# Cross-attention by pairs of heads, with 64-row score products on the two halves of TensorE's array

## The reference

```python
x = x + xattn(layernorm(x), ctx, ctx, Wq, bq, Wk, bk, Wv, bv)   # the changed part
x = x + attn(layernorm(x), w_in, ...)                           # 16 heads of 32, position bias
x = x + ffn(layernorm(x), Wg, W1, W2, W3)                       # 8 experts, top 2

def xattn(Q, K, V, ...):           # H = 16 head slots, DK = 64; D = 512, so 8 heads
    q, k, v = proj(Q, Wq, bq), proj(K, Wk, bk), proj(V, Wv, bv)
    scores = einsum('bhqd,bhkd->bhqk', q, k) / sqrt(DK)
    out = einsum('bhqk,bhkd->bhqd', softmax(scores), v)
    return out.transpose(0, 2, 1, 3).reshape(B, -1, D_MODEL)
```

## Time and profile before

| | us |
|---|---|
| median of 3 runs | 1715.8 (1715.32 to 1717.26) |
| the profiled execution | 1716.57 |
| its span, first to last instruction | 1714.7 |
| TensorE busy | 1664.1 |
| VectorE busy | 1478.4 |
| ScalarE busy | 1282.5 |
| GpSimd busy | 407.4 |
| start, up to the loop's first scores | 50.3 |
| the loop's chunks with projections | up to 1345.5 |
| last chunk without projection | 1345.5 to some 1369 |

### The profile page before, as it was taken

The page is one execution under the profiler, slowest core; times in us unless marked ns, Lnnn a source line. Parts: engine busy times, 40 slices in busy tenths (PEclk is TensorE's granted clock), DMA queues, the critical chain, the costliest instruction groups (busy, mean ns, idle before and its releaser), DMA issues.

```text
span 1714.7 us, 39194 instructions
## 1 busy us (share of the span) xinstructions
PE 1664.1 (97%) x13412; PEld 1000.6 (58%) x13412; DVE 1478.4 (86%) x2349; ACT 1282.5 (75%) x3167; POOL 407.4 (24%) x500
## 2 busy tenths in 40 slices
PE   6999999999999999999999999999999687999998
PEld 3555555555555555555555555555555465777776
DVE  6999999999999999999999999999999846776765
ACT  4788888888888888888888888888888634655554
POOL 3233233232232232332232332332332100000000
PEclk9999999999999999999999999999999875999999
DMA  6455555555555555554555555555564670465551
GB/s 240 78 127 125 108 122 104 124 115 116 128 105 122 107 123 125 106 125 100 128 122 108 124 104 122 114 119 125 108 124 81 112 240 1 149 219 186 211 192 50
DMA packets 442396, 215.93 MB, mean 126 GB/s; under 512 B 416736, under 2 KB 422880, under 8 KB 435568
## 3 DMA queue, kind: packets, MB, share of 16 engines
q1 hardware_dynamic: 442064, 215.07, 51.9%
q10 hardware_dynamic: 288, 0.27, 0.1%
HBM read 111.96 MB, written 0.56 MB: 66 GB/s over the span
## 4 chain that ended last, share of the span: by engine, by line
PE 95%; DVE 2%; ACT 1%; DMA 1%; issue 1%; POOL 0%; SPq 0%; DVEq 0%; ACTq 0%; POOLq 0%
PE ps_proj L864 59%; PE ps_s L829 10%; PE ps_proj L946 9%; PE ps_o L845 8%; PE ps_o L969 4%; PE ps_s L902 1%; PE ps_proj L882 1%; PE ps_proj L913 1%; DVE wsp L661 1%; DMA ctx_f<-ctxt_dram 1%; PE ps_o L889 0%; PE ps_o L813 0%; POOL ctx_s L305 0%; PE ps_proj L923 0%; PE ps_s L793 0%
## 5 line engine op out<-in xcount | busy, mean ns | idle before, releaser
L864 PE MATMUL ps_proj<-ctx_s,wk_s 128*128 128x512 f16 x2352 | 541.5, 380 | 9.1 <-POOL ctx_s L305 9.0
L864 PE MATMUL ps_proj<-wv_s,ctx_s 128*128 128x512 f16 x2352 | 539.3, 379 | 0.0
L305 POOL TENSOR_TENSOR ctx_s<-ctx_f,ctx_s 128x512 f16<-128x512 f32 x196 | 272.8, 1393 | 894.7 <-ACT ctx_s L355 894.7
L394 ACT ACTIVATE prob<-ps_s,nmax 128x256 f32<-128x256 f32 x784 | 364.9, 470 | 113.0 <-DVE nmax L587 101.9
L864 PEld LDWEIGHTS ps_proj<-ctx_s,wk_s 128*128 128x128 f16 x2352 | 217.6, 98 | 244.0 <-POOL ctx_s L305 9.4
L864 PEld LDWEIGHTS ps_proj<-wv_s,ctx_s 128*128 128x128 f16 x2352 | 217.0, 98 | 232.3
L580 DVE TENSOR_REDUCE cmax<-ps_s 128x2 f32<-128x512 f32 x392 | 269.4, 687 | 62.5 <-PE ps_s L829 55.6
L597 DVE SCALAR_TENSOR_TENSOR k_s<-ps_proj,bk_s,k_s 64x512 f16<-64x512 f32 x392 | 294.0, 750 | 12.2 <-ACT k_s L363 3.1
L606 DVE SCALAR_TENSOR_TENSOR p_s<-prob,p_s 128x512 f16<-128x512 f32 x392 | 268.7, 685 | 7.7 <-ACT p_s L387 1.6
L387 ACT ACTIVATE p_s<-prob 128x512 f16<-128x512 f32 x392 | 247.0, 630 | 4.9
L829 PE MATMUL ps_s<-k_s,q_s 128*128 128x256 f16 x1568 | 236.9, 274 | 4.4 <-ACT prob L394 4.2
(11 more groups left out here) (119 smaller groups left out, 1154.6 us busy)
## 6 DMA issues: line engine op xcount, KB each, us to landing
ctx_f<-ctxt_dram SPq DMA_DIRECT2D x49, 1024.0 KB, 5.3
wst<-w_dram SPq DMA_DIRECT2D x96, 512.0 KB, 4.2
pt_s<-p_s SPq DMA_TRANSPOSE x392, 3.1
w_in_sb<-w_in_dram SPq DMA_DIRECT2D x1, 3072.0 KB, 11.8
tisa<-tisa_scores SPq DMA_DIRECT2D x3, 1024.0 KB, 14.5
w_f<-wk_dram SPq DMA_DIRECT2D x1, 1024.0 KB, 7.5
w_f<-wv_dram SPq DMA_DIRECT2D x1, 1024.0 KB, 11.6
w_f<-wq_dram SPq DMA_DIRECT2D x1, 1024.0 KB, 13.4
```

The costliest lines, as they stand in the source:

```text
L305: pool.tensor_tensor(out=ctx_s[odd][1][:, t, :], in0=ctx_f[odd][:, t, :], in1=ctx_s[odd][0][:, t, :], op=ALU.subtract).then_inc(ctx_low, 1)
L394: ins = act.activation(prob[:, u % 4, r * HC:(r + 1) * HC], ps_s[:, u % 2, r * HC:(r + 1) * HC], ACT.Exp, bias=nmax[odd][:, col:col + 1], ...
L864: ins = pe.matmul(ps_proj[:, u % 4, :], lhsT, rhs, start=(t == 0 and n == 0), stop=(t == DT - 1 and n == 2))
```

## The change

The loop goes by pairs of heads g = 0 to 3 (NG = 4) instead of heads.

- **K** stays as the projection leaves it: ScalarE writes the whole 128-row block's high part in one instruction, VectorE the low part in one, to a tensor of their own (k_s[i][0], k_s[i][1]). q is no longer doubled.
- **Scores** of a pair: for each row class, three products of 64 rows for each of the two heads, the heads in turn, head 0 in rows 0 to 63 into bank 0 of ps_s, head 1 in rows 64 to 127 into bank 1. That is 12 products of 64 rows for 8 of 128. A pair uses both banks, so the next pair's scores wait for all its exponentials.
- **Softmax**: one max and one nmax of four columns, four exponentials in a row, one P high and one P low of 1024 columns. prob and p_s have two buffers for four. P high and P low of a pair stand in the pair's own step, behind its exponentials (before: in the next step).
- **Transposes**: two DMA transposes per pair, the high and the low part of both heads, the high one behind P high already. PV_LAG is 2 pairs.
- **Projections**: two blocks per step, 2g behind the scores and 2g+1 behind P·V; their high and low parts are placed to match.

```diff
-PV_LAG = 5
+NG = NB // 2
+PV_LAG = 2
 # SyncE
-                sp.wait_ge(p_low, NB * c + u + 1)
-                sp.sem_inc(may_turn, 1)
-                sp.dma_start_transpose(pt_s[:, u, :, :, :].rearrange("p k b q -> p (k b) q"),
-                                       p_s[:, u % 4, :, :].rearrange("p k c -> p (k c)")).then_inc(turned_p[u], 16)
+                for k, split in enumerate((p_high, p_low)):
+                    sp.wait_ge(split, NG * c + g + 1)
+                    sp.sem_inc(may_turn, 1)
+                    sp.dma_start_transpose(pt_s[:, g, k, :, :], p_s[:, g % 2, k, :]).then_inc(turned_p[g], 16)
 # ScalarE, K high
-                    act.activation(k_s[odd][0:64, 2 * g, :], ps[0:64, :], ACT.Identity, bias=bk_s[0:64, g:g + 1])
-                    act.activation(k_s[odd][64:128, 2 * g + 1, :], ps[64:128, :], ACT.Identity,
-                                   bias=bk_s[64:128, g:g + 1]).then_inc(proj_high, 1)
+                    act.activation(k_s[odd][0][:, g, :], ps, ACT.Identity, bias=bk_s[:, g:g + 1]).then_inc(proj_high, 1)
 # ScalarE, the new step
+                for g in range(NG):
+                    pc, pg = (c, NB - 1) if g == 0 else (c + 1, 2 * g - 1)
+                    if exists(pc, 0):
+                        proj_highs(pc, pg, odd if g == 0 else 1 - odd)
+                    if exists(c, 2):
+                        ctx_highs(c + 2, odd, (g,))
+                    if exists(c, -1) and g == 0:
+                        alphas(c - 1, 1)
+                    if exists(c, 0):
+                        act.wait_ge(nmax_done, NG * c + g + 1)
...
+                        for b in range(2):
+                            for r in range(2):
+                                col = 4 * g + 2 * b + r
+                                ins = act.activation(prob[:, g % 2, (2 * b + r) * HC:(2 * b + r + 1) * HC],
+                                                     ps_s[:, b, r * HC:(r + 1) * HC], ACT.Exp, bias=nmax[odd][:, col:col + 1],
+                                                     scale=LOGIT_SCALE, accum_out=lsum[odd][:, col:col + 1])
+                        ins.then_inc(exp_done, 1)
+                    if exists(c, 1):
+                        proj_highs(c + 1, 2 * g, 1 - odd)
+                    if exists(c, 0):
+                        act.wait_ge(exp_done, NG * c + g + 1)
...
+                        act.activation(p_s[:, g % 2, 0, :], prob[:, g % 2, :], ACT.Copy, scale=P_SCALE).then_inc(p_high, 1)
+                        if g == 1:
+                            alphas(c, 0)
 # VectorE, the new step: max, nmax, then
+                    pc, pg = (c, NB - 1) if g == 0 else (c + 1, 2 * g - 1)
                     if exists(pc, 0):
+                        proj_lows(pc, pg, odd if g == 0 else 1 - odd)
                     for half, (dc, dodd) in ((1, (c - 1, 1 - odd)), (0, (c, odd))):
+                        if g == (0 if half else 1) and exists(dc, 0):
...
                             dve.tensor_tensor(dmax[:, cols], nmax[dodd][:, cols], nmax[1 - dodd][:, cols],
                                               ALU.subtract).then_inc(dmax_done, 1)
+                    if exists(c, 1):
+                        proj_lows(c + 1, 2 * g, 1 - odd)
+                    if exists(c, 0):
+                        dve.wait_ge(p_high, NG * c + g + 1)
+                        dve.scalar_tensor_tensor(out=p_s[:, g % 2, 1, :], in0=prob[:, g % 2, :], scalar=P_SCALE,
+                                                 in1=p_s[:, g % 2, 0, :], op0=ALU.mult, op1=ALU.subtract).then_inc(p_low, 1)
+                    if g in (0, 2) and exists(c, -1):
+                        half, n = g // 2, 2 * (c - 1) + g // 2
...
                         dve.tensor_tensor(acc, acc, ps_o[:, half, :], ALU.add).then_inc(added, 1)
 # TensorE, scores
-                        for r in range(2):
-                            for part in range(2):
-                                ins = pe.matmul(ps_s[:, u % 2, r * HC:(r + 1) * HC], q_s[part][:, u, r * P:(r + 1) * P],
-                                                k_s[odd][:, u, r * HC:(r + 1) * HC], start=(part == 0), stop=(part == 1))
+                        if g >= 1 or after(c, -1):
+                            pe.wait_ge(exp_done, NG * c + g)
+                        for r in range(2):
+                            for n, (a, b) in enumerate(THREE):
+                                for head in range(2):
+                                    rows = slice(DK * head, DK * head + DK)
+                                    ins = pe.matmul(ps_s[:, head, r * HC:(r + 1) * HC], q_s[a][rows, g, r * P:(r + 1) * P],
+                                                    k_s[odd][b][rows, g, r * HC:(r + 1) * HC], start=(n == 0), stop=(n == 2))
+                        ins.then_inc(s_done, 1)
+                    project(c, odd, 2 * g)
...
+                    project(c, odd, 2 * g + 1)
```

More of the change, by code:

```diff
@@ L61, in after, with back @@
     return not isinstance(c, int) or c + n >= least
-def back(c, u, lag, per=NB):
+def back(c, u, lag, per=NG):
     return (c, u - lag) if u >= lag else (c - 1, u - lag + per)
@@ new lines, in split_q, with proj_lows @@
+                ins = dve.tensor_tensor(q_s[1][:, :, :], q_f[:, :, :], q_s[0][:, :, :], ALU.subtract)
+                ins.then_inc(q_ready, 1)
+            def proj_lows(c, g, odd):
+                dve.wait_ge(proj_high, NB * c + g + 1)
+                ps = ps_proj[:, g % 4, :]
+                if g < 4:
+                    dve.scalar_tensor_tensor(out=k_s[odd][1][:, g, :], in0=ps, scalar=bk_s[:, g:g + 1], in1=k_s[odd][0][:, g, :],
+                                             op0=ALU.add, op1=ALU.subtract).then_inc(proj_low, 1)
+                else:
+                    dve.tensor_tensor(v_s[odd][1][:, g - 4, :], ps, v_s[odd][0][:, g - 4, :],
+                                      ALU.subtract).then_inc(proj_low, 1)
@@ L575, in step @@
             def step(c, odd):
[L576 removed]
+                for g in range(NG):
                     if exists(c, 0):
[L579 to L580 removed]
+                        dve.wait_ge(s_done, NG * c + g + 1)
+                        dve.tensor_reduce(cmax[:, g % 2, :], ps_s[:, :, :].rearrange("p b (r k) -> p (b r) k", r=2), AX,
@@ L603, in step @@
-                    tc, tu = back(c, u, 1)
-                    if exists(tc, 0):
-                        dve.wait_ge(p_high, NB * tc + tu + 1)
-                        dve.scalar_tensor_tensor(out=p_s[:, tu % 4, 1, :], in0=prob[:, tu % 4, :], scalar=P_SCALE,
-                                                 in1=p_s[:, tu % 4, 0, :], op0=ALU.mult, op1=ALU.subtract).then_inc(p_low, 1)
+                        proj_lows(pc, pg, odd if g == 0 else 1 - odd)
                     for half, (dc, dodd) in ((1, (c - 1, 1 - odd)), (0, (c, odd))):
-                        if u == (0 if half else 4) and exists(dc, 0):
+                        if g == (0 if half else 1) and exists(dc, 0):
@@ L815, in project_q, with project @@
                 ins.then_inc(q_done, 1)
+            def project(c, odd, u):
+                if not exists(c, 1):
+                    return
+                if u == 0:
+                    pe.wait_ge(ctx_low, DT * (c + 2))
+                if isinstance(c, int) and c == -1 and u in (0, 4):
+                    pe.wait_ge(w_split, 1 + u // 4)
+                if u >= 4 or after(c, 0):
+                    pe.wait_ge(proj_low, NB * c + NB + u - 3)
+                cs = ctx_s[1 - odd]
+                for t in range(DT):
+                    for n, (a, b) in enumerate(THREE):
+                        if u < 4:
+                            lhsT, rhs = wk_s[a][:, t, u * P:(u + 1) * P], cs[b][:, t, :]
+                        else:
+                            lhsT, rhs = cs[b][:, t, (u - 4) * P:(u - 3) * P], wv_s[a][:, t, :]
+                        ins = pe.matmul(ps_proj[:, u % 4, :], lhsT, rhs, start=(t == 0 and n == 0),
+                                        stop=(t == DT - 1 and n == 2))
+                ins.then_inc(proj_done, 1)
@@ L867, in step @@
-                    if isinstance(c, int) and c == -1 and u == 1:
+                        if vg % 2 == 0 and after(vc, -1):
+                            pe.wait_ge(added, 2 * vc + vg // 2 - 1)
+                        for head in range(2):
+                            u = 2 * vg + head
+                            for r in range(2):
+                                col = (u % 4) * 2 * DK + r * DK
+                                for i in range(2):
+                                    tile = 2 * r + i
+                                    for n, (a, b) in enumerate(THREE):
+                                        ins = pe.matmul(ps_o[:, vg // 2, col:col + DK], pt_s[:, vg, a, 4 * head + tile, :],
+                                                        v_s[vodd][b][:, tile, u * DK:(u + 1) * DK],
+                                                        start=(i == 0 and n == 0), stop=(i == 1 and n == 2))
```

162 lines of the change are left out of this document (44 added, 118 removed).

## The result

| | before | after |
|---|---|---|
| median of 6 runs each on one chip, us | 1715.8 (1715.32 to 1717.26) | 1723.42 (1722.25 to 1724.74) |
| profiled execution, its span | 1716.57, 1714.7 | 1723.75, 1722.0 |
| TensorE, VectorE, ScalarE busy | 1664.1, 1478.4, 1282.5 | 1661.5, 1090.8, 1095.7 |
| first scores of the loop | 50.34 | 50.55 |
| first scores of the last chunk | 1345.52 | 1344.51 |

A forecast was written before the change was run, and what follows sets the result against it. TensorE was taken to bound the kernel before and after, with the other engines just hidden. +2 us over the loop and +9 at the end gave +11 on the median of 1715.8: 1727 us, range 1706 to 1800.

The forecast's parts named there:

- The switches: TensorE's score bursts: each change between full and 64-row products costs 0.10 us, 0.20 per burst, eating the gain.
- Rival 2: Score bursts on TensorE: shape changes cost near zero, so the kernel gets faster, 1706 us; chance 0.14.
- The offset of the second half: Score burst on TensorE: 0.02 us added for the array's second half, within a burst of 0.88 against 0.875.
- The halves overlap: Scores on TensorE: 12 products of 64 rows take 6 slots, 0.656 us for 0.875, saving 0.219 per pair.
- The ring: Loop cycle max, nmax, exponentials, K/V high, P high, P low, next max: 26.3 to 26.7 us per chunk, under TensorE's 27.0.
- Meetings of nmax with GpSimd: VectorE's nmax held up by GpSimd multiplications in the loop: 0.3 to 0.6 us per chunk of a possible 1.65.
- rival 1: In the loop, the ring of ScalarE and VectorE replaces TensorE as the bound: 28.5 us per chunk, 1798 us; chance 0.27.
- A late pair without cost: Loop: a pair may be late once free; 5.9 us of other TensorE work against 3.4 leaves 2.2 us of cover.
- The transposes: DMA transposes, two per pair: about five us of cover before P·V needs P low, so no cost.
- The last chunk: No projection hides the ring there: 26.4 us from first scores to the last P low's end, against 18.0, so +8.4.
- the 0.7 by which the ring was to be late: Last chunk: 0.7 us of ring lateness counted in the 26.4 us to the end of the last P low.
- The last P·V: End of the last chunk: 24 products instead of 12 at the half clock, some 0.06 us each, +0.7.

The follow-up runs named there:

- the first experiment: Changed kernel with score products ordered three of head 0, then three of head 1 per row class, instead of heads in turn: 1725.21 us.

## Why the prediction came out as it did

Predicted 1727.0, faster/same/slower at 0.12/0.13/0.75; measured 1723.4, slower. The sum was +2 in the loop and +9 at the end; measured −1.2 and +8.2, with +0.3 at the start and behind.

- **The switches, 0.10 a side.** Right, and the step on which the sign hung: 0.10 in and 0.10 out in the trace, 0.107 and 0.105 from the runs that added and removed one. Rival 2 falls.
- **The offset of the second half, 0.02.** Too much: both halves start within a hundredth. That is the loop's miss: a burst of 0.87 instead of 0.88, and so per pair a hair less than the 0.875 removed instead of 0.01 more; the loop came out a little shorter where it was to be a little longer. Over 192 pairs a hundredth is 2 us, most of the 3.2 between +2 and −1.2. The term was priced right in kind and set a hundredth or two too high.
- **The halves overlap.** Right, and more robust than I had thought: the first experiment, which should have taken it away, didn't.
- **The ring, 26.3 to 26.7 clean.** At its lower edge: 26.4 as read in one chunk with its brush, 26.2 to 26.3 clean by the three runs with an extra max. Inside it K high costs 0.57, since P high starts that long after it, and not 0.70; the other steps are within 0.03.
- **Meetings of nmax with GpSimd, 0.3 to 0.6 per chunk.** Fewer: 4 x (194 − 160) ns = 0.14 in the mean. The walk through the chunk had the right places: 0.24 instead of 0.16 at the first pair, a near miss at the third; it missed a small one at the fourth (0.23 in some chunks). But its argument that the meeting thins out when the ring lags was wrong, and this was an argument against rival 1. A slowdown of rival 1's kind, the ring in TensorE's place, was 0.08 us away: an extra 0.14 per pair brought it on, at +35 us. The prediction had left the third pair open ("possibly"), and no step of it worked out whether they meet there; that they don't was luck.
- **A late pair without cost.** The prediction has 2.2 us of cover after one late pair; its own terms, 5.9 less 3.4, give 2.5. Nothing here tests it alone, and no sum uses it.
- **The transposes, nothing.** TensorE waits for none in the loop (it is busy throughout). Right.
- **The last chunk, 26.4 to the end of P low, +8.4.** Measured 25.5 (1344.51 to 1370.01), +7.5. The steps were right: 5.62 predicted, 5.64 measured. Two terms of the sum were too high: the 0.7 by which the ring was to be late (its max starts right behind the first burst), and 0.2 of the first scores.
- **The last P·V, +0.7.** Right: 1.48 for 24 products, 0.83 for 12 before, +0.65.

So the fall in VectorE's and ScalarE's work had no effect because neither bound the kernel; TensorE's saving of 0.22 per pair was eaten by two changes of shape; and folding two steps into one, with nothing left to hide it in the last chunk, made the difference of the medians.

## What to carry to other kernels

When products are cut to a part of the array so that two run side by side, add 0.2 us for each burst before counting the gain, and make bursts long: at twelve products it was all gone, at twenty-four half of it was left. When work moves from one step into another, sum the ring that it closes from start to start, and give it a margin larger than the longest GpSimd instruction that can meet a small VectorE one in it; the mean of the small one tells whether they meet. Work hidden in a loop is paid for once, where the loop runs out.

## What the runs showed of the hardware

- Products on a free half of the array are started ahead of earlier queued ones on the busy half: with three queued before them in the same hundredth, with six after 0.23 us. So the order of products within a burst matters little, as long as the halves take turns every three.
- Each change between 64-row and 128-row f16 products costs 0.105 to 0.107 us at the full clock, the same as between the 32-row and the full ones of the earlier trace rows.
- A VectorE instruction of four columns takes 0.16 us or, beside a GpSimd multiplication in SBUF, 1.05. An extra 0.14 us per step of the ring turned the one into the other in 47 of 49 chunks.
